# Inverse and level products of a delta-rule layer by tiles of 32 tokens instead of 64, with every engine's order rewritten

## The reference

```python
q = _causal_dwconv_silu(_l2norm(x @ Wq), conv_q)      # the same for k; v has no norm
g_forget = -exp(A_log) * softplus(x @ Wfa @ Wfb + dt_bias)
beta = sigmoid(x @ Wb)
def step(Sst, inp):                                   # over 512 tokens, per batch and head
    Sst = Sst * exp(gt)[..., :, None]
    err = vt - einsum('bhk,bhkv->bhv', kt, Sst)
    Sst = Sst + bt * kt[..., :, None] * err[..., None, :]
    ot = einsum('bhk,bhkv->bhv', qt, Sst)
x = x + (rmsnorm(attn) * sigmoid(x @ Wga @ Wgb)) @ Wo
```

## Time and profile before

| | us |
|---|---|
| median of 3 runs (lowest, highest) | 1009.48 (1007.05, 1011.78) |
| the profiled execution | 1013.73 |
| its span | 1011.9 |
| TensorE busy in the span | 949.9 (94%) |
| VectorE busy | 812.7 (80%) |
| ScalarE busy | 708.2 (70%) |
| GpSimd busy | 73.9 (7%) |

### The profile page before, as it was taken

How to read it: one execution, slowest core, us unless ns; L and a number is a source line. 1 busy time by engine, 2 the same in 40 slices (tenths; PEclk the granted TensorE clock), 3 DMA queues, 4 the chain that set the end, 5 groups by cost and what they waited for, 6 DMA issues and landing times.

```text
span 1011.9 us, 34566 instructions
## 1 busy us (share of the span) xinstructions
PE 949.9 (94%) x15274; PEld 721.6 (71%) x15274; DVE 812.7 (80%) x1707; ACT 708.2 (70%) x1556; POOL 73.9 (7%) x179
## 2 busy tenths in 40 slices
PE   4888699999999999999999999999999998999986
PEld 3534367777777777777777777777777777788774
DVE  5577679889888888889888898888888888777644
ACT  2376658887787778787778787877877787545441
POOL 7000000000000000000000000000000000000010
PEclk9898789999999999999999999999999999999999
DMA  6100010100000101200001000200000000000001
GB/s 164 49 1 13 29 31 31 41 13 13 13 3 2 31 31 31 72 13 13 13 2 29 21 17 28 82 13 3 13 13 13 13 13 13 13 13 3 3 2 42
DMA packets 29033, 24.14 MB, mean 24 GB/s; under 512 B 4626, under 2 KB 24276, under 8 KB 28884
## 3 DMA queue, kind: packets, MB, share of 16 engines
q1 hardware_dynamic: 28884, 21.94, 7.9%
HBM read 20.82 MB, written 1.11 MB: 22 GB/s over the span
## 4 chain that ended last, share of the span: by engine, by line
PE 87%; DVE 5%; ACT 4%; POOL 2%; issue 1%; POOLq 0%; DVEq 0%; ACTq 0%
PE psum L824 17%; PE psum L847 10%; PE psum L888 8%; PE psum L870 8%; PE psum L879 7%; PE psum L947 6%; PE psum L834 3%; PE psum L925 3%; PE psum L830 3%; PE psum L919 3%; PE psum L912 3%; PE psum L905 3%; PE psum L839 2%; PE psum L854 2%; PE psum L898 2%; PE psum L936 2%
## 5 line engine op out<-in xcount | busy, mean ns | idle before, releaser
L824 PE MATMUL psum<-hT,gw 128*128 128x512 f32 x384 | 189.9, 621 | 1.7 <-DVE pairs L1275 0.9
L847 PEld LDWEIGHTS psum<-kq,ks 128*64 128x64 f32 x3072 | 106.3, 139 | 74.8 <-issue 44.0
L1231 DVE SCALAR_TENSOR_TENSOR qkv<-pad,chan,qkv 128x512 f32<-128x512 f32 x192 | 135.7, 754 | 0.3
L847 PE MATMUL psum<-kq,ks 128*64 128x64 f32 x3072 | 124.0, 227 | 8.8 <-DVE tot L1269 4.5
L1257 DVE TENSOR_TENSOR kq<-kq,tot 128x512 f32<-128x512 f32 x160 | 110.3, 689 | 25.0 <-PE psum L847 25.0
L824 PEld LDWEIGHTS psum<-hT,gw 128*128 128x128 f32 x384 | 69.1, 197 | 64.3 <-issue 61.0
L1275 DVE COPY_PREDICATED pairs<-masks,psum 128x256 f32<-128x256 uint8 x192 | 102.1, 532 | 4.1 <-PE psum L847 4.1
L870 PE MATMUL psum<-tmat,pairs 64*64 64x32 f32 x2560 | 102.3, 220 | 2.9 <-ACT tmat L556 2.5
L870 PEld LDWEIGHTS psum<-tmat,pairs 64*64 64x64 f32 x2560 | 89.5, 135 | 18.9 <-issue 11.5
L888 PE MATMUL psum<-pairs,fmat 64*64 64x32 f32 x2560 | 101.8, 220 | 0.9 <-DVE fmat L1242 0.9
L888 PEld LDWEIGHTS psum<-pairs,fmat 64*64 64x64 f32 x2560 | 90.0, 136 | 9.1 <-issue 5.8
(11 more groups left out here) (163 smaller groups left out, 1695.0 us busy)
## 6 DMA issues: line engine op xcount, KB each, us to landing
bb<-beta_rows SPq DMA_DIRECT2D x32, 256.0 KB, 3.3
gw<-in_L_attn_Wq SPq DMA_DIRECT2D x16, 128.0 KB, 2.2
gw<-in_L_attn_Wk SPq DMA_DIRECT2D x16, 128.0 KB, 2.3
gw<-in_L_attn_Wv SPq DMA_DIRECT2D x16, 128.0 KB, 2.2
gwo<-in_L_attn_Wo SPq DMA_DIRECT2D x4, 512.0 KB, 5.8
x<-in_L_attn_hidden_states SPq DMA_DIRECT2D x4, 256.0 KB, 4.4
gfb<-in_L_attn_Wfb SPq DMA_DIRECT2D x16, 64.0 KB, 2.1
ggb<-in_L_attn_Wgb SPq DMA_DIRECT2D x4, 256.0 KB, 4.9
```

The lines of the kernel that those rows point to most:

```text
L824: last = eng.matmul(two(bank[to]), gw[:, t, kt, hh * D:(hh + 1) * D], two(hT[:, kt])[:, :, h * PW:(h + 1) * PW], start=(kt == 0), stop=(kt ...
L847: last = eng.matmul(o[rows(b), :, u], ks[:, p, tokens(b, u)], half(kq[:, p, :, tokens(b, u)], h, 1), start=True, stop=True)
L1231: last = eng.scalar_tensor_tensor(out=piece(t, i), in0=src, scalar=tap_weight(t, tap, i), in1=piece(t, i), op0=ALU.mult, op1=ALU.add)
```

## The change

Level products 0 to 4, the first turn, and steps 1 to 4 of the inverse are computed by 32 x 32 blocks. Each of their groups has 16 matmuls instead of 8, each on half the weight columns and half the moving columns, and four of them (two batches, two halves j) use four different 32-column tiles of the array. The last step (l = 5) keeps its 8 matmuls but contracts over 32 tokens. Level 5 is as before.

What the blocks no longer write must not be read: VectorE clears the first 256 columns of all eight PSUM banks once at the start, and GpSimd clears two 32-partition strips of `tt` in each slot (`clear_turned`), which `solve` waits for.

The assignment of PSUM banks is new, and the order of the steps in `slot(t)` is new on TensorE, VectorE and ScalarE; on GpSimd the clears are added.

```diff
-L_BANK = (2, 0, 2, 0, 1, 0)
+L_BANK = (7, 1, 0, 3, 2, 6)
...
+            def clear_turned(p):
+                for b in range(B):
+                    last = eng.memset(tt[quarter(b, 1), p, :].rearrange("p (u i) -> p u i", i=C)[:, :, 0:QUARTER], 0.0)
+                return last
...
+                    after(turned4_ready, n1 + 1)
+                    clear_turned(q).then_inc(turned_cleared, 1)
...
+                per = QUARTER // (2 * h)
                 for u in range(G):
                     for b in range(B):
-                        last = eng.matmul(o[rows(b), :, u], ks[:, p, tokens(b, u)],
-                                          half(kq[:, p, :, tokens(b, u)], h, 1), start=True, stop=True)
+                        for j in range(2):
+                            at = slice(u * P + b * C + j * QUARTER, u * P + b * C + (j + 1) * QUARTER)
+                            to = slice(b * C + j * QUARTER, b * C + (j + 1) * QUARTER)
+                            last = eng.matmul(o[to, :, u, j * per:(j + 1) * per], ks[:, p, at],
+                                              half(kq[:, p, :, at], h, 1), start=True, stop=True)
...
+            def block_products(o, l, left, right, upper):
+                h = LEVELS[l]
+                per = QUARTER // (2 * h)
+                for u in range(G):
+                    for b in range(B):
+                        for j in range(2):
+                            last = eng.matmul(o[quarter(b, j), u, j * per:(j + 1) * per], block_of(left, b, u, j),
+                                              half(block_of(right, b, u, j), h, upper), start=True, stop=True)
                 return last
...
             def inverse_turned(p, l):
                 h = LEVELS[l]
                 o = bank[TT_BANK[l]][:, 0:HC].rearrange("p (u n t) -> p u n t", u=G, t=h)
+                if l < NL - 1:
+                    return block_products(o, l, fmat[:, l - 1], tt[:, p], 1)
                 for u in range(G):
                     for b in range(B):
-                        last = eng.matmul(o[rows(b), u], cell(fmat[:, l - 1], b, u), half(cell(tt[:, p], b, u), h, 1),
-                                          start=True, stop=True)
+                        last = eng.matmul(o[rows(b), u], cell(fmat[:, l - 1], b, u)[QUARTER:C],
+                                          half(cell(tt[:, p], b, u), h, 1)[QUARTER:C], start=True, stop=True)
...
+            eng.memset(psum[:, :, 0:UC], 0.0)
...
+                    after(turned5_ready, n1 + 1)
+                    after(turned_cleared, n1 + 1)
+                    solve(q).then_inc(u_done, 1)
```

More of the change, by code:

```diff
@@ L35 @@
 C = 64
+QUARTER = P // 4
 NCH = S // C
@@ L860, in first_natural @@
                     for b in range(B):
-                        last = eng.matmul(cell(bank[T0_BANK][:, 0:UC], b, u), cell(tt[:, p], b, u), id64[rows(b), 0:C],
-                                          start=True, stop=True)
+                        for j in range(2):
+                            last = eng.matmul(block_of(bank[T0_BANK][:, 0:UC], b, u, j), block_of(tt[:, p], b, u, j),
+                                              block_of(id64, b, 0, j), start=True, stop=True)
+                return last
+            def block_products(o, l, left, right, upper):
+                h = LEVELS[l]
+                per = QUARTER // (2 * h)
+                for u in range(G):
+                    for b in range(B):
+                        for j in range(2):
+                            last = eng.matmul(o[quarter(b, j), u, j * per:(j + 1) * per], block_of(left, b, u, j),
+                                              half(block_of(right, b, u, j), h, upper), start=True, stop=True)
                 return last
@@ L867, in inverse_y @@
                 o = bank[Y_BANK[l]][:, 0:HC].rearrange("p (u n t) -> p u n t", u=G, t=h)
+                if l < NL - 1:
+                    return block_products(o, l, nmat[:, l], tmat, 0)
                 for u in range(G):
                     for b in range(B):
-                        last = eng.matmul(o[rows(b), u], cell(nmat[:, l], b, u), half(cell(tmat, b, u), h, 0),
+                        last = eng.matmul(o[rows(b), u], cell(nmat[:, l], b, u)[0:QUARTER], half(cell(tmat, b, u), h, 0)[0:QUARTER],
                                           start=True, stop=True)
@@ L876, in inverse_natural @@
                 o = bank[TM_BANK[l]][:, 0:HC].rearrange("p (u n t) -> p u n t", u=G, t=h)
-                for u in range(G):
-                    for b in range(B):
-                        last = eng.matmul(o[rows(b), u], cell(tt[:, p], b, u), half(cell(fmat[:, l - 1], b, u), h, 0),
-                                          start=True, stop=True)
-                return last
+                return block_products(o, l, tt[:, p], fmat[:, l - 1], 0)
             def inverse_turned(p, l):
@@ L957, in slot @@
                 n2 = t - 2
-                if 0 <= n1 < NCK:
-                    inverse_turned(q, 2).then_inc(turned2_done, 1)
+                if 0 <= n2 < NCK:
+                    after(us_ready, n2 + 1)
+                    queries_new(p).then_inc(o_done, 1)
+                    if n2 == NCK - 1:
+                        ln_turn(2, 0)
+                if 0 <= n1 < NCK:
+                    after(summed1, n1 + 1)
+                    inverse_natural(q, 1).then_inc(natural1_done, 1)
+                if 0 <= n2 < NCK:
+                    if n2 >= 31:
+                        after(x_added, n2)
+                    new_state(n2).then_inc(s_done, 1)
@@ L1281, in slot @@
                 im4 = t + 4
+                im3 = t + 3
                 n0 = t
@@ L1396, in _ @@
             ln_centre(2, 0)
-            for t in range(NCK - 2, NCK + 1):
+            for t in range(NCK - 2, NCK):
                 slot(t)
             ln_scale(2, 0)
+            slot(NCK)
             slot(NCK + 1)
```

573 lines of the change are left out of this document (294 added, 279 removed).

## The result

| | before | after |
|---|---|---|
| median (lowest to highest), 20 runs each | 1009.64 us (1007.05 to 1017.31) | 1007.52 us (996.3 to 1015.42) |
| ratio, 95% interval | | 0.9937 (0.9909 to 0.9965) |
| the profiled execution | 1013.73 us | 1011.17 us |
| TensorE busy | 949.9 us | 924.1 us |
| MATMUL records | 15,274 | 24,490 |

A forecast was written before the change was run, and what follows sets the result against it. TensorE's own list was taken to bound the slot. 3.06 - 1.56 - 0.2 = 1.3 us a slot, 35 us over 27 slots plus 3 in the last four, gave a median of 971.5 us; own range 945 to 995.

The forecast's parts named there:

- The small group's price: TensorE's 18 blocked groups a slot: 0.30 us each instead of 0.47, a gain of 3.06 us a slot.
- The change of shape: TensorE's switches between tile shapes: 13 more a slot at 0.12 us each, costing 1.56 us a slot.
- The wait of 0.2 us at the seam of the slots: TensorE waits for VectorE's first sum before `inverse_natural`(1) where two slots meet: 0.1 to 0.3 us, 0.2 taken.
- The clears: GpSimd's two memsets a slot, 0.1 to 0.25 us each, and VectorE's 1.8 us at the start: cost nothing.
- The undisturbed slot: One slot of the main stretch: 1.3 us shorter, from 27.5 to some 26.2 us.
- VectorE takes the place: Rival: groups get cheap but VectorE's waits do not shrink, slot stays 27.5 us, time 1000 to 1009; 10%.
- 27 x 1.3 = 35 us: The 27 slots from 131.8 to 871.6 us each gain 1.3 us, 35 us together.
- the granted clock should stay at 1.00: Expected sign: TensorE's clock stays at the upper of its two levels, 2.4 GHz.
- the last four: The last four slots, 871.6 to 963.0 us, partly waiting for other engines: gain 0.7 us each, 3 us together.
- Every record its own 0.029 us: Rival: each small matmul record holds TensorE's list 0.029 us, 10.0 us a slot more, about 1320 us; 14%.
- between 0.235 and 0.94: Bounds in us for a blocked group: half a set of two per set of four, or 0.029 for each of 32 records.

The follow-up runs named there:

- e3: The changed kernel's order, banks and clears, but level products, first turn and inverse products by 64 x 64 cells as before; 1078.07 us, ratio 1.0679 to before.
- e8: The changed kernel with weight loads after the first groups and beta rows from the third unit cut to 2 partitions; 984.79 us, ratio 0.9745 to before.
- e6: Blocks of 32 as in the changed kernel, but order and banks of the kernel before, without GpSimd's clears; 1055.70 us, ratio 1.0421 to before.
- e5: Not the layer: streams of TensorE's groups alone, some beside bulk loads or with pauses; without loads 0.91 us per blocked group, 0.47 per 64 x 64 group.
- e4: The changed kernel with its weight loads spread over the slot and the output weights' scaling two slots later; 995.21 us, ratio 0.9878 to before.
- e9: The changed kernel with two long filler matmuls in each of the last four slots, where TensorE waits; 999.72 us, ratio 0.9889 to before.

## Why the prediction was wrong

*What held.* The small group's price: 0.27 us against 0.30 taken. The change of shape: 0.10 by the timeline and 0.15 by e3 (1.8 us / 12, less if a wait is in it) against 0.12. The wait of 0.2 us at the seam of the slots did not come. The clears were free as far as the trace shows (nobody waits for them); no run goes without them alone. The undisturbed slot is 26.0 us in the mean of the first eight against 27.4 of before, a gain of 1.5 us with 1.3 forecast. VectorE did not take the place: it is 91% busy in the slot of 26.19 (23.82), and TensorE still has 25.93.

*What failed.* Not a term of the sum but the step from the slot to the whole, "27 x 1.3 = 35 us", with the sentence that nothing TensorE waits for sets the slot's length and the last line, "the granted clock should stay at 1.00". It was true of the old list. The 27 slots gained 10.3 us (735.4 to 725.1) instead of 35, and the last four lost 9.2 instead of gaining 3. The prediction put the supply of instructions at nothing, without a word on it. The runs show in its place: 192 blocks instead of 120, 25.4 us of idle in the 27 slots instead of 5.4 (16.8 of them with the releaser "issue"), and 39.4 us at the lower clock instead of 6.8; with the loads out of the way (e8) the same list takes 705.6 us, where 735.4 less 35 makes 700.4. How the 25 us between 10.3 and 35 divide into standing still and the lower clock isn't settled by a run. The scatter of the kernel's runs gives an estimate: from 0.961 to 0.939 in mean clock a run spends some 46 us more at the lower level and takes 19 us longer, 0.4 us for each. By that the 32.6 us more at the lower level would be 13 of the 25 us, with the reserve that pauses and a low clock come together.

The tail was not cleared up. The versions with 27 to 34 us at the lower clock there take 100.6 to 103.3 us, those with 3 to 17 us take 95.1 to 97.0 (e3 apart, which has no blocks), so the clock is likely some 5 us of the loss. At least 3.7 us against 91.4 are left in every version, in e6 with the old order too, and weren't traced.

*The rivals.* "Every record its own 0.029 us" is refuted as it stood: 32 records take 0.27 us, 8 ns each. But it asked the right question, whether records can come faster than they had so far, and gave an answer that was wrong for the wrong span: there is a floor, 14 ns per instruction or 0.91 us per group, for the long run only (e5). The Trainium skill's page TensorE: Matmul & The Clock Gate, section Back-to-back issue gap, gives a floor of about 25 ns between starts; by it the group would be 0.80 us (an estimate), and the burst of 0.27 us undercuts it threefold. I bounded the price of a group between 0.235 and 0.94 and never asked how long a burst may last. "VectorE takes the place" would have given the measured time (1000 to 1009) with 10%, for a reason that no row bears out.

*Could it be seen before?* The page had "q8 instruction: 120, 1.97" and the diff doubled the records of 18 groups a slot. 1.97 MB over 1012 us gives 8.4 us per block on average, and the new list has one per 5.3. What the trace of before didn't have was the least distance of two blocks under load; it had 3.5 us as the smallest. That would have made a warning, since 3.5 us for 256 instructions would be 0.88 us for a blocked group of 64 instructions, if no block came sooner.

## What to carry over

Where a change halves matmuls and doubles their number, count instructions as well as array time: in this case two blocks of 256 instructions of TensorE start at least 3.2 us apart, 3.7 in a long run, so short groups are cheap only in bursts between long ones. Bulk loads are better spread than bunched (e4 gained 6 to 12 us). Idle time whose releaser is "issue", in the middle of a group, is the mark of it; look then at the granted clock right behind. In a stretch in which TensorE waits anyway, long matmuls in the waits are worth a try: in e9's profile the stretch got shorter, though no whole time shows the gain. And take several profiles of a kernel that scatters: the same 27 slots took 725.1 us in one version's profile and 716.3 in another's.

## What the hardware showed that I had not expected

32-bit matmuls on 32 x 32 tiles run at 0.27 us for 32 records with their 32 weight loads, 4.2 ns per instruction; 207 of them in e5 before the first stop. Within a bunch of loads (1.75 MB in 13 us) two instruction blocks started 7.5 us apart (404.68 and 412.15), where 4.1 is the median, and the engine needed another 1.3 to 1.4 us from the landing of the block to the next matmul (351.96 to 353.26, 413.11 to 414.52). In e5 the clock stood at 1.2 GHz for 92 us, through the stream of blocked groups in which TensorE paused 24 times without a semaphore wait in the trace, and for 32 us of a 64 x 64 stream without any pause, behind one of 0.65 us.
